# Attention of the second layer: the product with values moves ahead of the transposes of the probabilities

## What is computed

```
Q, K, V = relu(x @ Wq + bq), relu(x @ Wk + bk), relu(x @ Wv + bv)     # 16 heads of width 8
scores = einsum('bqhd,bkhd->bhqk', Qh, Kh) / sqrt(8)                   # masked causally
attn   = softmax(scores) * query_mask
out    = einsum('bhqk,bkhd->bqhd', attn, Vh).reshape(B, T, U) + x
out    = gamma * (out - mean) / sqrt(var + EPS) + beta
```

## Time and profile before

| | |
|---|---|
| median of 3 runs | 1016.11 (1016.07 to 1016.4) |
| span of the profiled execution | 1016.5 |
| TensorE busy in it | 977.0 (96%) |
| VectorE, ScalarE, GpSimd busy | 876.8, 831.3, 471.2 |
| first and last transpose at L1798 | 714.6 and 926.0 |
| granted TensorE clock, mean | 0.997 of 2.4 GHz |

### The profile page before, as it was taken

The page is one execution under the profiler, slowest core; times in us unless marked ns, Lnnn a source line. Parts: engine busy times, 40 slices in busy tenths (PEclk is TensorE's granted clock), DMA queues, the critical chain, the costliest instruction groups (busy, mean ns, idle before and its releaser), DMA issues.

```text
span 1016.5 us, 25956 instructions
## 1 busy us (share of the span) xinstructions
PE 977.0 (96%) x8939; PEld 789.2 (78%) x8939; DVE 876.8 (86%) x3718; ACT 831.3 (82%) x2232; POOL 471.2 (46%) x541
## 2 busy tenths in 40 slices
PE   7999999999999999999989999999999999999897
PEld 6898888888888989743268988888777777776566
DVE  6777989898989888799998899889988888896985
ACT  6888888888888888887797878776887888886786
POOL 2334545454545463606810112102887888893041
PEclk9999999999999999999999999999999999999999
DMA  9000000000000000000000000000000000000002
GB/s 376 35 2 2 2 2 2 2 2 2 2 2 2 2 2 2 2 1 0 1 1 1 1 1 1 1 11 11 23 23 23 23 23 23 23 3 1 1 2 84
DMA packets 8723, 18.31 MB, mean 18 GB/s; under 512 B 1296, under 2 KB 5648, under 8 KB 8208
## 3 DMA queue, kind: packets, MB, share of 16 engines
q1 hardware_dynamic: 8592, 16.65, 4.9%
HBM read 10.36 MB, written 2.10 MB: 12 GB/s over the span
## 4 chain that ended last, share of the span: by engine, by line
PE 79%; DVE 9%; ACT 6%; POOL 3%; issue 3%; DMA 0%; DVEq 0%; ACTq 0%; POOLq 0%
PE PB L245 8%; PE PB L246 8%; PE PB L247 8%; PE PB L341 6%; PE PB L396 6%; PE PB L379 6%; PE PB L1798 5%; PE PB L1195 3%; PE PB L1770 3%; PE PB L1197 3%; PE PB L1196 3%; PE PB L1815 3%; PE PB L428 2%; PE PB L429 1%; PE PB L430 1%
## 5 line engine op out<-in xcount | busy, mean ns | idle before, releaser
L371 POOL TENSOR_TENSOR W<-W,small 128x512 f32<-128x512 f32 x128 | 138.5, 1082 | 216.3 <-DVE small L365 216.3
L360 ACT ACTIVATE W<-W,small 128x128 f32<-128x128 f32 x512 | 198.8, 390 | 29.6 <-DVE small L351 29.0
L245 PE MATMUL PB<-RR_s 128*128 128x256 f32 (+3 forms) x568 | 184.4, 325 | 3.5 <-issue 1.9
L246 PE MATMUL PB<-RR_s 128*128 128x256 f32 (+3 forms) x568 | 176.8, 311 | 0.0
L247 PE MATMUL PB<-RR_s 128*128 128x256 f32 (+3 forms) x568 | 176.7, 311 | 0.0
L351 DVE CUSTOM_DVE_ANT_0 W<-PB,W 128x128 f32<-128x128 f32 x512 | 117.3, 284 | 39.1 <-PE PB L341 38.1
L1786 POOL TENSOR_TENSOR AR_s<-AR_s,small 128x512 f32<-128x512 f32 x128 | 129.3, 1040 | 15.9 <-DVE small L1779 15.8
L1169 ACT ACTIVATE AR_s<-PB,W 128x512 f32<-128x512 f32 (+2 forms) x160 | 100.5, 629 | 28.5 <-PE PB L247 22.1
L245 PEld LDWEIGHTS PB<-RR_s 128*128 128x128 f32 x568 | 108.6, 191 | 11.1 <-issue 4.2
L1183 DVE TENSOR_TENSOR RR_s<-AR_s,RR_s 128x512 fp32r<-128x512 f32 (+2 forms) x160 | 100.4, 636 | 17.1 <-ACT RR_s L1174 13.8
L1779 DVE CUSTOM_DVE_ANT_0 AR_s<-PB,W 128x128 f32<-128x128 f32 x512 | 111.0, 286 | 2.6 <-PE PB L1770 0.9
(11 more groups left out here) (385 smaller groups left out, 2437.0 us busy)
## 6 DMA issues: line engine op xcount, KB each, us to landing
W<-in_w SPq DMA_DIRECT2D x1, 5809.5 KB, 25.5
W<-in_w SPq DMA_DIRECT2D x2, 1024.0 KB, 7.2
out<-XT SPq DMA_DIRECT2D x8, 256.0 KB, 2.3
XF<-in_xT SPq DMA_DIRECT2D x3, 512.0 KB, 10.9
W<-AR_s SPq DMA_DIRECT2D x16, 64.0 KB, 2.1
AR_s<-AR_s SPq DMA_DIRECT2D x16, 64.0 KB, 2.1
QS<-AR_s SPq DMA_DIRECT2D x12, 64.0 KB, 2.1
KR<-AR_s SPq DMA_DIRECT2D x12, 64.0 KB, 2.1
```

The source lines that it names most:

```text
L245: nc.tensor.matmul(out, lh, rh, start=True, stop=False)
L246: nc.tensor.matmul(out, ll, rh, start=False, stop=False)
L360: e = nc.scalar.activation(SS[r][:, hl], SS[r][:, hl], ACTF.Exp, bias=mx[r][:, h:h + 1], scale=-1.0, accum_out=rc[r][:, h:h + 1])
L371: nc.gpsimd.tensor_tensor(s3, s3, over(rc[r], 2, [128, 4, 128]), ALU.mult).then_inc(s_nrm, 1)
```

## The change

In `plan5` and `pe_attend2` the product with values of row q - 2 moves from behind `pe_v5` to directly behind the scores of row q, ahead of all transposes of the step. In `act_attend2` its copy `act_o5(q - 2)` moves from behind the first exponential `act_exp5(4q)` to ahead of the first two copies of transposes. The wait for `s_pa` at q == 2 moves with it. No instruction is added or removed. DVE, POOL and the DMA queue keep their order. Since `plan5` changes too, which output has which of banks 4 and 5, and which copy each writer waits for, changes as well.

```
@@ plan5
             for q in range(NB5):
+                if q >= 2:
+                    passes5(("o", q - 2), 4, s_o5, q - 1)
                 plan_T5(4 * q - 4)
                 plan_T5(4 * q - 3)
                 plan_asides(q, TURNED)
                 if q + 1 < NB5:
                     passes5(("v", q + 1), 6, s_vt, q + 2)
-                if q >= 2:
-                    passes5(("o", q - 2), 4, s_o5, q - 1)
                 plan_asides(q, PROJECTED)
@@ pe_attend2
+                if q >= 2:
+                    pe_PV5(q - 2)
                 if q:
                     pe_T5(4 * q - 4)
                     pe_T5(4 * q - 3)
                 steps_of(turned, q)
                 if q + 1 < NB5:
                     pe_v5(q + 1)
-                if q >= 2:
-                    pe_PV5(q - 2)
                 steps_of(projected, q)
@@ act_attend2
                 if q:
                     act_exp5(4 * q - 1)
+                if q == 2:
+                    act.wait_ge(s_pa, added(NJ - 1))
+                if q >= 2:
+                    act_o5(q - 2)
+                if q:
                     act_pt5(4 * q - 4)
                     act_pt5(4 * q - 3)
                 step_of(beside, 4 * q)
                 step_of(beside, 4 * q + 1)
                 act_exp5(4 * q)
-                if q == 2:
-                    act.wait_ge(s_pa, added(NJ - 1))
-                if q >= 2:
-                    act_o5(q - 2)
                 step_of(beside, 4 * q + 2)
```

More of the change, by code:

```diff
@@ L2632, in act_attend2 @@
                 act_exp5(4 * q)
[L2633 to L2636, removed]
                 step_of(beside, 4 * q + 2)
```

## The result

The changed kernel takes 1030.22 us (median of 4 runs, 1029.8 to 1031.46), the kernel before beside it 1016.25 (4 runs): a ratio of 1.0129, 95% interval 1.0117 to 1.0141, slower by some 13 us. The forecast was 1026.2, with 1020 to 1030 as range: the direction and the main mechanism were right, a second wait was missing from the sum, and the median lies 0.2 above the range.

What follows compares the result with a forecast made beforehand. TensorE's queue was taken to bound the kernel. Five rounds at 1.57 give 7.9, the ten other steps 2.2, together 10.1 on the median 1016.1: 1026.2 us, range 1020 to 1030.

Steps and rivals of the forecast that it cites:

- What bounds the kernel: In regular steps TensorE's queue has nothing to spare; a wait counts in full unless it replaces another; 26.5 per round.
- The bank turn: In banks 4 and 5, second transposes wait for the product's copy until y + 1.85: 0.43 in each of 30 steps.
- What it takes back: The product no longer stands behind `pe_v5`: saves 0.17 in steps with q mod 4 = 1 and 3, nothing in 0.
- At 2: 0.43: Steps with q mod 4 = 2 grow by 0.43, the wait for the product's copy.
- The product behind an apply: At q mod 4 = 3, ACT's chain with apply allows the next product only after 7.22: 0.45 for that step.
- Sum for a round: Steps with q mod 4 = 1, 2, 3, 0 add 0.26, 0.43, 0.45, 0.43: together 1.57, so 26.5 becomes 28.1.
- Step 7: The long wait, about 2, moves from T(4q-1) to the next product; step 7 grows 0.1, slow clock stays.
- The rival: New wait smaller, or step 7's slow clock goes, saving 1.6 to 1.8: 1020 to 1023; chance 0.14.
- DVE "hidden": Transposes are done before DVE's third and fourth groups of maxima need them, with 0.22 left, so no cost.
- The clock falling again and again: Rival: new waits lower the clock, each of six rounds losing about 1.7: 1036; chance 0.10, shared with other queueing.

Runs made afterwards that it cites:

- other pair of banks: Changed kernel with the product's output written to banks 6 and 7 instead of 4 and 5: 1021.47 us, ratio 1.0038 to the kernel before.
- the trial with tokens ahead: Changed kernel with TensorE's order scores, first transposes, tokens or gamma, product, second transposes, values; ACT copies tokens before the product: 1013.38 us, ratio 0.9958.
- product between the two groups: Changed kernel with the product between the first and second transposes of a step, ACT's copies in the same order: 1018.74 us, ratio 1.0014.
- turned asides and values between: Changed kernel with tokens or gamma, then values, between first and second transposes; tokens' copy ahead of the second transposes' copy: 1019.63 us, ratio 1.0029.
- the copy made twice: Changed kernel with ACT copying the product a second time, the bank free only after that: 1051.32 us, ratio 1.0331 to the kernel before.
- values between: Changed kernel with only the projection to values moved between the first and second transposes, ahead of tokens and gamma: 1032.96 us, ratio 1.0154.

## Why the prediction was right, and where it fell short

**What bounds the kernel.** Right. TensorE's queue sets the pace, and a wait in it counts in full: 30 waits grew by 0.63 each and the time by 20.

**The bank turn.** Right to a hundredth: y + 1.01, y + 1.86 for y + 1.85, 12.6 in total for 12.9. The other pair of banks took this wait away and 9 of some 13 us with it.

**What it takes back.** Too small. I had counted 0.17 in every second step and nothing in the others. In step 14 the product started 0.42 behind the first values load (805.36 to 805.78), where what follows the values starts 0.22 behind them if it is wide (`select` in the trial with tokens ahead, 803.99 to 804.21); behind the scores the product costs no such gap: it starts 1.10 after them (806.61 to 807.71), and so did the first transposes before, as one more row of that trace beside 810.26 shows, the scores of step 15 in the timeline of PEld:

```profile
809.16 0.98 PEld L1770 LDWEIGHTS PB<-AR_s,W 32*128 32x128 f32 x32 [0.17 <-issue]
```

So each regular step gains another 0.20. Steps 1 and 3 show it: +0.09 and +0.03 for the forecast +0.26 and, on TensorE alone, +0.26. Step 0, measured with three normalizations left out, shows it too: 0.43 - 0.20 = 0.23.

**What stood in the product's old place.** This is the step of the prediction that failed: "At 2: 0.43" takes the product out from between values and `select` and asks nothing about the writer behind it. `select` waits for the tokens' copy, two turns back in banks 6 and 7. I looked for new waits only in banks 4 and 5, whose order the edit changes; that of 6 and 7 is the same, but the time between its writers is not. The wait costs 0.71 in each step with q mod 4 = 2, so this step grew by 1.00 where 0.43 was forecast (0.43 + 0.71 - 0.20 = 0.94). In steps 2 and 6 no `select` stands, and `factors` and `b1` wait for the same copy, 0.7 and 0.8.

It is tempting to blame ACT's queue, where the tokens' copy now stands behind the product's. The timelines of step 14 speak against it, each counted from the tokens' first weight load (L1906):

| kernel | tokens' copy starts | `select` starts | of which it waited |
|---|---|---|---|
| before | 0.84 | 1.87 | none |
| changed | 0.80 | 1.45 | 0.71 |
| product in the other pair of banks | 0.84 | 1.49 | 0.76 |
| product between the two groups | 0.80 | 1.45 | 0.71 |
| turned asides and values between | 0.80 | 1.45 | 0.33 |
| tokens ahead of the product | 0.81 | 2.26 | none |

The copy starts at the same distance in all six, wherever it stands on ACT. Where ACT waits for four transposes, its copy starts 0.69 after their first weight load (809.57 to 810.26), so the queue costs some 0.1 of it at most. What differs is the work on TensorE between tokens and `select`: values alone leave a wait of 0.71 to 0.76, four transposes more leave 0.33, and with the product too nothing is left.

**The product behind an apply.** Right in kind. ACT's chain lets the product go only late; it appears in step 0 as 0.5, not as 0.2 in step 3, because TensorE reached the end of step 3 earlier than I had it (6.80 for 7.03). Both steps together: +0.78 for the forecast +0.88.

**Sum for a round.** 0.09 + 1.00 + 0.03 + 0.75 = 1.87 for 1.57; the two errors of size, -0.2 in each step and +0.71 in one, partly cancel.

**Step 7.** The wait of 2.1 moved to the product of step 8, as forecast. "So I leave the slow clock behind it in" was wrong for this execution: no stretch below 1.00 followed it, and steps 7 and 8 gained 1.18 where +0.5 was forecast. The rival had this in it, for 1.6 to 1.8.

**DVE "hidden".** Right in the rounds, wrong in step 28, which has few helpers. There gamma's transposes, pushed back by product and wait, come late for DVE's addition, and the last maxima stand behind it. The timeline of PEld:

```profile
912.86 0.98 PEld L1770 LDWEIGHTS PB<-AR_s,W 32*128 32x128 f32 x32 [1.26 <-DVE small L1779]
```

Step 29's scores wait 1.26 for them, most of the 1.53 of step 28. With gamma ahead of the product the step took 5.53.

**The clock falling again and again.** It did not. By the rule of the Trainium skill, TensorE: Matmul & The Clock Gate, section "A second HAM failure mode: psum-queue depth-cycling", frequent short idles between groups of matmuls can make the clock swing; this trace does not agree for waits of the weight loads of 0.4 to 0.7, of which a round has seven: the window of 28.4 above shows 1.00, and the profiled run's mean is 0.996.

**What stays open.** The medians above differ by 14.0 and the profiled spans by 12.0. With the 1.3 by which a span lies below its time, the profiled execution before took about 1017.8, 1.6 above its median, and the one after is the fastest of its four, 0.4 below its median; that makes up the 2.0. The execution before is one of the longer of its kind: in the run against itself the spans of this kernel were 1013.9 to 1017.2. Why executions of one kernel differ by 3 was not looked into.

## What to carry to other kernels

When outputs rotate through a pair of PSUM banks, write down for each writer whose copy it waits for, before and after the edit, since moving one output changes the partner of others. Then look at the place that the moved work has left, for the pairs whose order stays too: what stood behind it now comes earlier and may ask for a bank whose copy, though no later than before, is not yet done. A wait that is small beside a step counts in full, and as often as the loop runs, if the engine's queue has no slack. The better place was neither first nor last: a group of other work on either side of the product, so each copy has time before its bank is asked for.

## What the runs showed of the hardware

A product made of 32 matmuls with 32-column weights costs the queue an extra 0.20 behind the 128-column product for the values, and nothing extra behind the scores, also made of thin pieces: 0.42 against 0.22 from one first weight load to the next behind the values, 1.10 in both cases behind the scores. Behind the tokens' transposes it is the same: 0.64 to the product (801.95 to 802.59, with tokens ahead), 0.43 to the values (809.96 to 810.39, changed kernel).

The granted clock did not follow the length of a wait. Seven of the traces have a wait of the weight loads of about 2 in step 7 or 8. Within the next microseconds the clock fell to 0.50, over two microseconds, after 2.14 (kernel before), 2.15 (the same kernel again) and 2.11 (the copy made twice). It stayed at 1.00 after 2.10 (changed kernel), 1.96 (the other pair of banks), 2.11 (values between) and 2.11 (turned asides and values between). Ahead of its fall TensorE was busy for 2.3 of the microseconds from 756 to 760 in the kernel before; in the last of the others it was busy for 2.05 of those from 760 to 764, and the clock stayed. What decides was not found.
